# A macaron block on one core: wide products whose result nothing reads, x loaded twice, the last numerators without DRAM

## The chip, the core and the metric

The kernel is one program on one NeuronCore of a Trainium2 chip. The metric is the device time of one execution, in microseconds (us). A profile of one execution gives the start and length of each instruction; times inside it are counted from the start of the span.

## The reference

x is (4, 1024, 128) in float32, so there are 4096 tokens of 128 numbers. Three layers add to x in turn:

```python
x = x + 0.5 * ffn(layernorm(x))
x = x + attn(layernorm(x))
x = x + 0.5 * ffn(layernorm(x))

def ffn(x):                       # 8 experts, each token goes to one
    top1 = argmax(softmax(x @ router_w + router_b))
    for i in range(8):
        a, g = split(x @ w1[i] + b1[i])          # 128 -> 2 x 512
        y = (a * sigmoid(g)) @ w2[i] + b2[i]     # 512 -> 128
        out += where(top1 == i, y, 0)
    return out

def attn(x):                      # 16 heads of 8, scores plus phi_bias
    p = softmax(q @ k.T * 8**-0.5 + log(exp(-|pos_i - pos_j|) + 1e-8))
    return (p @ v) @ w_proj + b_proj
```

## The kernel before

The work is in five parts, one after another on the core: the first routing (`phase_first`), the first experts, the preparation of attention (`phase_attend`), attention (`phase_attention_last`, 64 heads; its end holds the second routing), and the second experts. Both experts parts are `phase_experts`. Each engine has a program of its own, and semaphores order them.

**Routing.** The 4096 tokens are 32 tiles of 128, taken as 8 groups of 4 tiles (512 tokens) and 4 chunks of 2 groups. For a group, VectorE takes mean and variance, ScalarE (for some groups VectorE) writes the normalised tokens into `xn`, TensorE turns four tiles (`turn`), ScalarE copies them to `xT`, and TensorE multiplies them with the router's weights, which are only 8 columns wide (`use`, L275). For a chunk, VectorE picks each token's expert in a row of small dependent steps with drains between them; TensorE counts the tokens above each token (`rank_chunk`, L285 and L287); VectorE writes two arrays of marks (L242 and L251), and TensorE sums them in eight products into a table of which token stands in which place (`enter_chunk`, L305). The last chunk's steps are `Router.place_last`, which gives its marks in two halves. `count_tokens` (L293) gives the tokens of each expert; `plan_tiles` turns these into the 39 tiles of the experts part: starts of experts, `slot`, `eid`, and, when ScalarE has copied the table (`copy_table`, L314) and TensorE has picked from it (`pick_tokens`, L323), the token numbers `idx`. The gathers of the experts part wait for `idx` and for all stores of `stored` (`load_first_rows`). ScalarE's queue holds `halve_bias` (L373) in front of `copy_table`; it waits until all expert weights and `b2` have landed. `run_up` (L380) is RUNUP products of 128x256 float32 that nothing reads, after the pick. A product in float32 shows as two instructions in the trace.

**Rows and DMA.** `g.rows` keeps 256 numbers per token: the normalised token, and behind it x (`g.xt`). A store to DRAM takes both together (`store_rows`, L98). In `phase_first`, x is loaded straight into `g.xt`, that is in pieces of 512 bytes: groups 0, 1, 2 and 3, 6 and 7 by SyncE's queue, 4 and 5 by ScalarE's. Then SyncE issues the marks, and group by group the weights `w1` and `w2` of an expert and the store of the group's rows, each store after the group is normalised, and last `b2`. The second routing has the same loop, without the loads of x.

**The end of attention.** Two heads at a time end in `osum` in SBUF (32-row blocks: 8 rows of numerators and one denominator for each quarter of the tokens; two heads side by side). SyncE writes them to `weighted_sums` in DRAM and later reads numerators (`load_num`) and denominators (`load_den`) of a batch back in the layout that the projection needs. For the last two heads the denominators already go from `osum` to `den` directly (`load_last_den`, L1055). Their numerators go to DRAM (L1232), SyncE waits for that, and reads them back (L1061). VectorE multiplies numerators and reciprocals (`divide_last`, L1503) for groups 6 and 7, TensorE projects (`project`, L1375), VectorE adds to x (`new_x`, L1508), and the routing steps of groups 6 and 7 follow. The chunks 1, 2 and 3 of the second routing lie behind that in VectorE's program.

## Time and profile before

| what | value |
|---|---|
| time, median of 3 runs | 1059.32 us (1057.64 to 1061.11) |
| the profiled execution's own time | 1058.07 us |
| its span, first to last instruction | 1056.2 us |
| TensorE busy | 977.1 us, 93% |
| VectorE busy | 899.5 us, 85% |
| ScalarE busy | 734.5 us, 70% |
| GpSimd busy | 357.5 us, 34% |
| DMA | 102.40 MB, mean 97 GB/s |

The first routing runs from the start of the span to about 52 us, the second from about 892 us to about 937 us. Busy shares are means over the whole span; the routing stages are read by themselves from the timeline.

### The profile page before, as it was taken

The numbers are of one execution on the slowest core, as the hardware profiler recorded it, in microseconds if no ns is written. First come the engines' busy times: TensorE is split into PE (matmuls) and PEld (weight loads), VectorE is DVE, ScalarE is ACT, GpSimd is POOL, SyncE is SP. The second block draws the span as 40 slices with busy tenths as digits, with TensorE's granted clock in tenths as the row PEclk, the third lists the DMA queues.
The fourth block names the chain that finished last, engine by engine and source line by source line (L and its number), as shares of the span: only waits on it lengthen the run. The fifth ranks groups of instructions, "written<-read, shape, count | busy, mean of one in ns | idle before, by whom it ended". The sixth has DMA issues, their size and how long they took to land. (4 is left out here: it accounts for less than half of the span.)

```text
span 1056.2 us, 34555 instructions
## 1 busy us (share of the span) xinstructions
PE 977.1 (93%) x11722; PEld 544.9 (52%) x11722; DVE 899.5 (85%) x1638; ACT 734.5 (70%) x1587; POOL 357.5 (34%) x495
## 2 busy tenths in 40 slices
PE   5899995969999999999999999999999989679997
PEld 4799993513333333333333333333333335569997
DVE  6778874779999999999999999999999988667886
ACT  4244442848888888888888888888888875234443
POOL 0067772202222222223222232222222242027775
PEclk9999996969999999999999999999999999679999
DMA  9532224752222222222222222222222343922221
GB/s 323 206 96 70 70 70 112 241 192 65 70 76 63 70 72 60 73 71 64 72 69 69 63 73 74 59 73 72 58 74 71 100 121 98 336 81 70 70 71 41
DMA packets 77898, 102.40 MB, mean 97 GB/s; under 512 B 15473, under 2 KB 55031, under 8 KB 77798
## 3 DMA queue, kind: packets, MB, share of 16 engines
q1 hardware_dynamic: 67830, 84.21, 26.6%
q0 software_dynamic: 6240, 14.44, 4.6%
q10 hardware_dynamic: 3760, 2.89, 0.9%
q8 instruction: 37, 0.61, 0.2%
q14 instruction: 31, 0.25, 0.1%
HBM read 70.61 MB, written 31.78 MB: 97 GB/s over the span
## 5 line engine op out<-in xcount | busy, mean ns | idle before, releaser
L1490 DVE TENSOR_REDUCE nmax<-psS 128x1 f32<-128x1024 f32 x507 | 595.7, 1218 | 36.7 <-PE psS L1326 29.3
L1672 ACT ACTIVATE big<-psE 128x512 f32<-128x512 f32 x1024 | 553.4, 598 | 95.6 <-PE psE L1311 93.1
L1311 PE MATMUL psE<-qop,kop 122*32 122x512 bf16 x4096 | 318.0, 384 | 5.0 <-ACT big L1672 3.6
L1761 POOL TENSOR_TENSOR big<-big,const 128x512 f32<-128x512 f32 x128 | 139.8, 1092 | 464.7 <-ACT big L1672 464.7
L1346 PE MATMUL psV<-big,vst 128*9 128x256 f32 x4096 | 265.6, 379 | 1.3
L1326 PE MATMUL psS<-maxop 32*128 32x512 bf16 x1014 | 174.6, 391 | 20.6 <-DVE nmax L1490 12.1
L1346 PEld LDWEIGHTS psV<-big,vst 128*9 128x9 f32 x4096 | 101.8, 90 | 116.3 <-issue 12.6
L1311 PEld LDWEIGHTS psE<-qop,kop 122*32 122x32 bf16 x4096 | 90.2, 95 | 130.7 <-ACT big L1672 59.5
L1326 PEld LDWEIGHTS psS<-maxop 32*128 32x128 bf16 x1014 | 47.7, 91 | 179.3 <-issue 109.1
L1028 ACT ACTIVATE sigb<-psGb,big 128x128 f32<-128x128 f32 x156 | 44.6, 368 | 59.2 <-PE psGb L953 59.2
L1028 ACT ACTIVATE siga<-psGa,w1sa 128x128 f32<-128x128 f32 x156 | 44.6, 369 | 58.4 <-PE psGa L953 58.4
L119 POOL DMA_INDIRECT xs<-stored_a,idx x39 | 38.1, 977 | 60.8 <-ACTq L386 49.2
L119 POOL DMA_INDIRECT xs<-stored_b,idx x39 | 38.0, 974 | 57.8 <-DVE idx L357 46.3
L930 POOL DMA_INDIRECT out_x<-yb,idx x39 | 44.3, 1136 | 25.7 <-issue 13.0
L930 POOL DMA_INDIRECT results<-ya,idx x39 | 44.9, 1151 | 23.7 <-issue 11.4
L1011 DVE SCALAR_TENSOR_TENSOR hidb<-psAb,big,sigb 128x128 f32<-128x128 f32 x156 | 43.6, 342 | 2.2 <-PE psAb L953 2.0
L1011 DVE SCALAR_TENSOR_TENSOR hida<-psAa,w1sa,siga 128x128 f32<-128x128 f32 x156 | 43.7, 342 | 1.0 <-ACT siga L1028 0.8
L969 PE MATMUL psYa<-w2a,hida 128*128 x312 | 41.5, 276 | 1.7 <-DVE hida L1011 1.6
L969 PE MATMUL psYb<-big,hidb 128*128 x312 | 41.6, 276 | 1.6 <-DVE hidb L1011 1.6
L953 PE MATMUL psGb<-xsTb,big 128*128 128x128 f32 x312 | 42.3, 280 | 0.7 <-ACT xsTb L1036 0.7
L953 PE MATMUL psGa<-xsTa,w1sa 128*128 128x128 f32 x312 | 41.5, 276 | 0.7 <-ACT xsTa L1036 0.7
L953 PE MATMUL psAb<-xsTb,big 128*128 128x128 f32 x312 | 42.0, 279 | 0.0
(213 smaller groups left out, 940.0 us busy)
## 6 DMA issues: line engine op xcount, KB each, us to landing
maxop<-qk_parts SPq DMA_DIRECT2D x256, 64.0 KB, 1.9
qop<-qk_parts SPq DMA_DIRECT2D x64, 144.0 KB
kop<-qk_parts SPq DMA_DIRECT2D x64, 144.0 KB
weighted_sums<-osum SPq DMA_DIRECT2D x64, 128.0 KB
qk_parts<-big SPq DMA_DIRECT2D x12, 384.0 KB, 3.4
w1a<-in_w SPq DMA_DIRECT2D x8, 516.0 KB, 7.6
big<-in_w SPq DMA_DIRECT2D x8, 516.0 KB, 6.9
stored_a<-rows SPq DMA_DIRECT2D x8, 512.0 KB, 7.7
```

Source lines behind the costliest of these rows:

```text
L119: pool.indirect_dma_start(out=g.xs[:, i % XBUF, :], out_offset=None, in_=d.stored[g.turn], in_offset=bass.IndirectOffsetOnAxis(ap=g.idx[:, ...
L930: pool.indirect_dma_start(out=to, in_=y[:, s, :], in_offset=None, bounds_check=NTOK - 1, oob_is_err=False, out_offset=bass.IndirectOffsetO ...
L953: last = nc.tensor.matmul(ps[:, c * P:(c + 1) * P], w1s[:, s, lo:lo + P], xsT[:, s, :], start=True, stop=True)
L969: last = nc.tensor.matmul(psY[1 - s][:, 0:D], hid[:, 1 - s, c * P:(c + 1) * P], g.w2[:, bass.ds(e * HID + c * P, P)], start=(c == 0), stop ...
L1011: last = nc.vector.scalar_tensor_tensor(out=hid[:, s, c * P:(c + 1) * P], in0=psA[s][:, c * P:(c + 1) * P], scalar=w1s[:, s, 2 * HID + c:2 ...
L1028: last = nc.scalar.activation(sig[:, s, c * P:(c + 1) * P], psG[s][:, c * P:(c + 1) * P], ACT.Sigmoid, bias=w1s[:, s, b:b + 1])
L1311: last = nc.tensor.matmul(psE[BANK[turn]][32 * c:32 * c + 32, :], kop[b][0:TROWS, lo:lo + 32], qop[b][0:TROWS, half * HALF:(half + 1) * HALF],
L1326: last = nc.tensor.matmul(psS[n % 2][:, half, :], maxop[b][lo:lo + SROWS, 0, qt % 4 * P:(qt % 4 + 1) * P], maxop[b][lo:lo + SROWS, 1, :], ...
L1346: last = nc.tensor.matmul(psV[32 * c:32 * c + VW, side:side + QUART], vst[(r + 1) % 2][:, k, :], prob[(r + 1) % 2][:, at_c:at_c + QUART], ...
L1490: nc.vector.tensor_reduce(nmax[r % 2][:, qt:qt + 1], psS[n % 2][:], AX.XY, ALU.max, negate=True).then_inc(s_max, 1)
L1672: nc.scalar.activation(prob[r % 2][:, lo:lo + HALF], psE[BANK[16 * (r % NBUF) + n]][:], ACT.Exp).then_inc(s_exp, 1)
L1761: nc.gpsimd.tensor_tensor(dst, dst, diag[:, 4 * h:4 * h + 4, :], ALU.mult).then_inc(s_diag, 1)
```

## The change

Five things change.

- **Unread products.** TensorE gets more products of 128x256 float32 whose result nothing reads. In the first routing: 7 at the start (on an array `fill` of zeros that GpSimd writes), one after each of 8 turns, one after each of 7 uses, then 2, 1, 4 and 1 around the last counts and table entries: 30. In the second: 13, on constants. RUNUP goes from 5 to 7.
- **Early x.** Groups 0 to 3 are loaded into an array `xq` of their own, in pieces of 2 KB or more, and are read from there. All loads of x are in SyncE's queue, the constants in one load behind groups 0 and 1. Behind the marks, the x of groups 0 to 3 is loaded again into `g.xt` (1 MB), and the store of group 0 waits for that.
- **Last numerators.** `load_last_num` moves the last two heads' numerators from `osum` to `num`, four DMAs by SyncE and four by GpSimd; `divide_last(7)` waits for GpSimd's. The last write to `weighted_sums`, the wait for it and the read back are gone.
- **Counting inside place_last.** Six small steps of `plan_tiles` (up to `at`) stand between the steps of `place_last`, which now holds `rank`, `near` and `split` too, and a wait for the counts.
- Waits of TensorE for constants are one, behind the first 7 products.

```diff
@@ -50,7 +50,8 @@
...
 LEAD = 2
-RUNUP = 5
+RUNUP = 7
+EARLY = 4
@@ -252,17 +253,30 @@
...
-    def place_last(self, dve, c):
+    def place_last(self, dve, c, p):
...
         h = CT // 2
+        self.rank(c)
+        dve.drain()
+        dve.wait_ge(p.s_cnt, 1)
+        self.near(c)
+        self.v.tensor_scalar(p.near[:, 0:E], p.counts[:, 0:E], float(P - 1) / 2, MAGIC, ALU.add, ALU.add)
+        self.v.memset(p.pad[:, 0:1], 0.0)
+        dve.drain()
+        self.split(c)
+        self.v.tensor_scalar(p.pad[:, 1:E + 1], p.near[:, 0:E], -MAGIC, None, ALU.add)
+        dve.drain()
...
         self.one_column(c)
+        self.v.tensor_tensor_scan(p.start[:], self.g.const[:, C_ONE:C_ONE + E + 1], p.pad[:], 0.0, ALU.mult, ALU.add)
...
         self.name(c)
+        self.v.tensor_tensor(p.mine[:, 0:E], p.start[:, 0:E], self.g.const[:, C_MASK:C_MASK + E], ALU.mult)
...
         dve.drain()
+        self.v.tensor_reduce(p.at[:], p.mine[:, 0:E], AX.X, ALU.add)
@@ -327,18 +341,6 @@
...
-    dve.wait_ge(p.s_cnt, 1)
-    nc.vector.tensor_scalar(p.near[:, 0:E], p.counts[:, 0:E], float(P - 1) / 2, MAGIC, ALU.add, ALU.add)
-    nc.vector.memset(p.pad[:, 0:1], 0.0)
-    dve.drain()
-    nc.vector.tensor_scalar(p.pad[:, 1:E + 1], p.near[:, 0:E], -MAGIC, None, ALU.add)
-    dve.drain()
-    nc.vector.tensor_tensor_scan(p.start[:], g.const[:, C_ONE:C_ONE + E + 1], p.pad[:], 0.0, ALU.mult, ALU.add)
-    dve.drain()
-    nc.vector.tensor_tensor(p.mine[:, 0:E], p.start[:, 0:E], g.const[:, C_MASK:C_MASK + E], ALU.mult)
-    dve.drain()
-    nc.vector.tensor_reduce(p.at[:], p.mine[:, 0:E], AX.X, ALU.add)
-    dve.drain()
@@ -402,7 +404,9 @@
...
             sem(n) for n in ("var", "std", "rs", "xn", "xa", "tp", "xT", "used"))
-        s_upto, s_rank, s_small, s_marks, s_ident = (sem(n) for n in ("upto", "rank", "small", "marks", "ident"))
+        s_upto, s_rank, s_small, s_marks, s_again, s_fill = (
+            sem(n) for n in ("upto", "rank", "small", "marks", "again", "fill"))
+        xq, fill = sb("xq", [P, 4 * EARLY, D]), sb("fill", [P, OFFS])
@@ -419,20 +423,30 @@
...
+        def load_early(eng, n, count):
+            eng.dma_start(xq[:, 4 * n:4 * (n + count), :].rearrange("p j d -> p (j d)"),
+                          d.x[:, n * HALF:(n + count) * HALF]).then_inc(s_src[n], 16)
+        def x_of(t):
+            return xq[:, t, :] if t < 4 * EARLY else xt[:, t, :]
...
         def _(sp):
-            load_x(sp, 0, 1)
-            sp.dma_start(g.const[:, 0:C_TRI], d.const[:, 0:C_TRI]).then_inc(s_ident, 16)
-            load_x(sp, 1, 1)
-            sp.dma_start(g.const[:, C_TRI:C_DIAG], d.const[:, C_TRI:C_DIAG]).then_inc(s_small, 16)
-            load_x(sp, 2, 2)
+            load_early(sp, 0, 1)
+            load_early(sp, 1, 1)
+            sp.dma_start(g.const[:, 0:C_DIAG], d.const[:, 0:C_DIAG]).then_inc(s_small, 16)
+            load_early(sp, 2, 2)
+            load_x(sp, 4, 2)
...
             sp.dma_start(g.marks[:], d.marks).then_inc(s_marks, 16)
+            sp.dma_start(xt[:, 0:EARLY * 4, :], d.x[:, 0:EARLY * HALF].rearrange("p (j d) -> p j d", d=D))\
+                .then_inc(s_again, 16)
...
                 if n == 0:
+                    sp.wait_ge(s_again, 16)
@@ -441,13 +455,14 @@
...
         def _(pool):
+            nc.gpsimd.memset(fill[:], 0.0).then_inc(s_fill, 1)
...
                 for j in range(lo, hi):
-                    nc.vector.bn_stats(stats[:, c, j, :], xt[:, CT * c + j, :])
+                    nc.vector.bn_stats(stats[:, c, j, :], x_of(CT * c + j))
@@ -466,7 +481,7 @@
...
                 for j in range(4):
-                    last = nc.vector.tensor_scalar(xn[:, j, 0:D], xt[:, j, :], mv[:, 0, j, 0:1], rstd[:, 0, j:j + 1],
+                    last = nc.vector.tensor_scalar(xn[:, j, 0:D], x_of(j), mv[:, 0, j, 0:1], rstd[:, 0, j:j + 1],
@@ -503,6 +518,9 @@
...
                 dve.drain()
+                if t == CHUNKS:
+                    router.place_last(dve, t - 1, plan)
+                    break
@@ -527,9 +545,6 @@
...
                     router.pick(t)
-                if t == CHUNKS:
-                    router.place_last(dve, t - 1)
-                    break
@@ -559,9 +574,16 @@
...
         def _(pe):
+            def unread(count, bank):
+                for _ in range(count):
+                    nc.tensor.matmul(bank[:, 0:OFFS], fill[:, 0:P], fill[:], start=True, stop=True)
+            pe.wait_ge(s_fill, 1)
+            unread(7, plan.counts)
+            pe.wait_ge(s_small, 3 * 16)
...
                 if n == 0:
-                    pe.wait_ge(s_ident, 16)
@@ -570,12 +592,13 @@
...
                 last.then_inc(s_tp, 1)
+                unread(1, plan.counts)
...
             def use(n):
-                if n == 0:
-                    pe.wait_ge(s_small, 3 * 16)
...
                 use_group(nc, pe, router, xT, n).then_inc(s_used, 1)
+                if n < groups - 1:
+                    unread(1, plan.counts)
@@ -596,10 +619,14 @@
...
             enter_chunk(nc, pe, router, 1)
+            unread(2, psT[1])
...
             count_tokens(nc, pe, router, plan)
+            unread(1, psT[1])
             enter_chunk(nc, pe, router, 2)
+            unread(4, psT[1])
             enter_chunk(nc, pe, router, 3)
+            unread(1, psT[1])
@@ -607,13 +634,12 @@
...
             act.dma_start(g.br[:], d.router_b.partition_broadcast(P)).then_inc(s_small, 16)
-            load_x(act, 4, 2)
...
                     k = n % 2 * 4 + j
-                    last = nc.scalar.activation(xn[:, 4 * n + j, 0:D], xt[:, 4 * n + j, :], ACT.Identity,
+                    last = nc.scalar.activation(xn[:, 4 * n + j, 0:D], x_of(4 * n + j), ACT.Identity,
@@ -1055,6 +1081,16 @@
...
+def load_last_num(eng, g, osum, quarters, landed):
+    for c in quarters:
+        for side in range(2):
+            lo = (HEADS - 2 + side) * DH
+            eng.dma_start(g.num[lo:lo + DH, (B - 1) % 2, c * QUART:(c + 1) * QUART],
+                          osum[32 * c:32 * c + DH, side * QUART:(side + 1) * QUART]).then_inc(landed, 16)
@@ -1148,7 +1184,7 @@
...
         s_aT_last = m.sem("s_aT_late")
-        s_pick, s_spread = m.sem("s_pick"), m.sem("s_spread")
+        s_pick, s_spread, s_num_late = m.sem("s_pick"), m.sem("s_spread"), m.sem("s_num_late")
@@ -1226,7 +1262,8 @@
...
                             load_last_den(sp, g, osum[s], side)
-                    for side in range(2):
+                        load_last_num(sp, g, osum[s], (0, 1), g.s_num_in[B - 1])
+                    for side in range(2 if at != N + 1 else 0):
@@ -1277,8 +1314,6 @@
...
             steps(sp, step, -3, N + 2)
-            sp.wait_ge(s_os[1], 16 * (N // 2))
-            load_num(sp, d, g, B - 1, HEADS - 2, HEADS)
@@ -1429,6 +1464,11 @@
...
             steps(pe, step, -2, N + 1)
+            def unread(count):
+                for _ in range(count):
+                    nc.tensor.matmul(psD[0][:, 0:OFFS], g.const[:, C_ONE:C_ONE + P], g.const[:, 0:OFFS],
+                                     start=True, stop=True)
@@ -1441,22 +1481,31 @@
...
             turn(4)
+            unread(1)
...
             use(4)
+            unread(1)
             use(5)
+            unread(2)
...
             pe.wait_ge(s_ev, N // 2)
+            unread(1)
...
             turn(6)
+            unread(1)
...
             use(6)
+            unread(1)
...
             enter_chunk(nc, pe, router, 1)
+            unread(2)
...
             enter_chunk(nc, pe, router, 2)
+            unread(3)
             enter_chunk(nc, pe, router, 3)
+            unread(1)
@@ -1497,7 +1546,9 @@
...
                 if n % 2 == 0:
-                    dve.wait_ge(g.s_num_in[B - 1], 2 * 16)
+                    dve.wait_ge(g.s_num_in[B - 1], 5 * 16)
+                else:
+                    dve.wait_ge(s_num_late, 4 * 16)
@@ -1580,6 +1631,9 @@
...
                 dve.drain()
+                if place == CHUNKS - 1:
+                    router.place_last(dve, place, plan)
+                    return
@@ -1601,9 +1655,6 @@
...
                 dve.drain()
-                if place == CHUNKS - 1:
-                    router.place_last(dve, place)
-                    return
@@ -1794,6 +1845,8 @@
...
             steps(pool, step, -1, 64)
+            pool.wait_ge(s_ev, N // 2)
+            load_last_num(pool, g, osum[(N // 2 - 1) % 2], (2, 3), s_num_late)
...

```

## Rows read from the trace of the kernel before

**Rows 1.** The page's slices of the span (40 of 26.4 us): TensorE's granted clock in tenths.

```profile
PEclk9999996969999999999999999999999999679999
```

**Rows 2.** Busy time by stretch, first routing: us, PE, PEld, DVE, ACT, POOL, PEclk, DMA share, GB/s.

```profile
4.00:10.00 6.00, 0.00 (x0) 0.00 (x0) 3.57 (x23) 0.41 (x2) 0.00 (x0) 1.00 1.06 302
10.00:39.00 29.00, 26.86 (x123) 24.69 (x124) 22.47 (x122) 15.87 (x39) 0.00 (x0) 1.00 1.03 398
```

**Rows 3.** Timeline, first routing, VectorE: start us, us, what [idle before, releaser].

```profile
7.70 0.88 DVE L450 BATCH_NORM_STATS2 stats_first<-rows 128x6 f32<-128x128 f32 x4 [2.10 <-DMA rows<-in_x]
```

**Rows 4.** Waits of VectorE in the first 52 us: total, times, longest.

```profile
DVE row_first L211 <- PE psL_first L287: 2.2, 3, 0.9
```

**Rows 5.** Timeline, end of the first routing and first experts tile.

```profile
40.63 1.06 ACT L373 ACTIVATE b2a<-b2a 128x1024 f32<-128x1024 f32 x1 [8.19 <-DMA b2a<-in_b]
...
44.91 1.93 PE L305 MATMUL psI_first<-hot_off_first,hot_col_first 128*128 128x256 f16 x8 [1.98 <-DVE hot_col_first L251]
...
45.28 0.17 DVE L331 TENSOR_SCALAR near_first<-psC_first 128x8 f32<-128x8 f32 x1
45.40 0.06 DVE L332 MEMSET pad_first<- 128x1 f32 x1
...
46.87 0.37 ACT L314 CAST table_first<-psI_first 128x256 f16<-128x256 f32 x1 [5.18 <-PE psI_first L305]
...
52.75 0.30 PE L961 MATMUL psXa<-const,xs 128*128 128x128 f32 x1 [1.06 <-DMA xs<-stored_a,idx]
...
55.86 1.13 DVE L1011 SCALAR_TENSOR_TENSOR hida<-psAa,w1sa,siga 128x128 f32<-128x128 f32 x4 [0.82 <-ACT siga L1028]
```

**Rows 6.** Groups by form, first 52 us, then 919 to 921 us: busy us, mean ns.

```profile
L275 PEld LDWEIGHTS psL_first<-wr,xT_first 128*128 128x128 f32 x64 | 14.1, 332 | 0.3 <-ACT xT_first L624 0.2
...
L380 PE MATMUL psI_first<-const 128*128 128x256 f32 x10 | 4.3, 613 | 0.0
...
L275 PEld LDWEIGHTS psE<-wr,xT_last 128*128 128x128 f32 x16 | 1.9, 191 | 0.0
```

**Rows 7.** Timeline, end of attention and start of the second routing.

```profile
892.23 2.05 PE L1375 MATMUL psS<-wproj,aT 128*128 128x128 f32 x16
...
892.98 1.33 SPq L1055 DMA_DIRECT2D den<-osum  x2
...
895.90 0.95 DVE L1496 RECIPROCAL rec<-den 128x128 f32<-128x128 f32 x1 [0.23 <-DMA den<-osum]
...
899.22 0.69 SPq L1061 DMA_DIRECT2D num<-weighted_sums  x1
...
904.18 1.28 DVE L1503 TENSOR_TENSOR aT<-num,psE 128x512 f32<-128x512 f32 x2 [5.40 <-DMA num<-weighted_sums]
...
904.92 3.50 PE L1375 MATMUL psS<-wproj,aT 128*128 128x128 f32 x16 [5.17 <-DVE aT L1503]
...
907.03 0.69 DVE L1508 TENSOR_TENSOR rows<-psS,rows 128x512 f32<-128x512 f32 x1 [0.91 <-PE psS L1375]
```

**Rows 8.** The page's groups: gathers issued by GpSimd, busy us, mean ns of one.

```profile
L119 POOL DMA_INDIRECT xs<-stored_a,idx x39 | 38.1, 977 | 60.8 <-ACTq L386 49.2
```

**Rows 9.** Busy time by stretch, second routing and start of the experts (columns as in rows 2).

```profile
904.00:927.00 23.00, 17.01 (x95) 14.90 (x96) 19.97 (x84) 7.27 (x17) 0.00 (x0) 0.65 1.02 396
...
935.30:938.70 3.40, 1.52 (x8) 0.88 (x6) 0.76 (x2) 0.27 (x1) 2.67 (x3) 1.00 0.26 77
938.70:942.10 3.40, 3.40 (x16) 3.40 (x17) 1.04 (x2) 1.14 (x4) 1.97 (x2) 0.50 0.37 96
```

**Rows 10.** Timeline, end of the second routing and first tile of the second experts.

```profile
929.23 1.06 ACT L373 ACTIVATE big<-big 128x1024 f32<-128x1024 f32 x1 [9.07 <-DMA big<-in_b]
...
932.31 0.37 ACT L314 CAST table_last<-psV 128x256 f16<-128x256 f32 x1 [2.02 <-PE psV L305]
...
937.97 0.30 PE L961 MATMUL psXb<-const,xs 128*128 128x128 f32 x1 [1.52 <-DMA xs<-stored_b,idx]
...
942.34 1.12 DVE L1011 SCALAR_TENSOR_TENSOR hidb<-psAb,big,sigb 128x128 f32<-128x128 f32 x4 [1.99 <-PE psAb L953]
```


## The prediction

> **What bounds the kernel now.** I read the page's slices first, then the two routing stretches by themselves, since the change touches only those. Between them TensorE is granted its full clock nearly everywhere [rows 1] and nothing is edited there. In the page's slices both routings look like a mix; the timeline shows one chain in each.
>
> First routing. Three things run side by side. The DMA engines are full from 4 to 39 us, at 302 GB/s up to 10 us, where x arrives in 512-byte pieces, and at 398 GB/s after it [rows 2]. VectorE is busy 22.47 of the 29 us from 10 to 39 and most of the rest is drains between short dependent steps; the waits that the profile names are 2.1 us for the second piece of x [rows 3] and 2.2 us for TensorE's ranks [rows 4]. TensorE is busy 26.86 of those 29 us [rows 2]. The granted clock says 1.00 there, but nothing had been recorded yet: a weight load of L275 takes 332 ns, and 191 ns in the second routing at a time when the clock was granted in full [rows 6]. So I read the whole first routing as run at 1.2 GHz.
>
> The stretch ends at ScalarE's copy of the table, at 46.87, and from there to the first turn of the experts, at 52.75, is a fixed tail of 5.9 us [rows 5]. What came last was the table (1.93 us of eight products from 44.91). But ScalarE's queue has a second gate: the halved bias waits for `b2`, the last weight to land, until 40.63 and takes 1.06 us. So the DMA side ends at 41.7, which leaves 5.2 us of slack [rows 5]. This is the number to watch.
>
> Second routing. VectorE stops for 5.40 us (898.8 to 904.18) for the last heads' numerators, which SyncE could ask for only at 899.22; TensorE stops with it for 5.17 us and then projects at 1.2 GHz, 3.50 us instead of the 2.05 us of the same sixteen instructions at 892.23 [rows 7]. After that VectorE is busy 19.97 of 23 us [rows 9], so it sets the pace up to the last marks. DMA is again full, 396 GB/s from 904 to 927 [rows 9], the bias is released at 929.23 and done at 930.3, and the copy follows at 932.31: only 2.0 us of slack [rows 10].
>
> **The last numerators.** Before, the denominators took 1.33 us for two issues from 892.98, and the reciprocal ran at 895.90, 1.6 us after the second issue ended [rows 7]. Four more issues by SyncE at 0.67 us each end at 897.0 and land at 898.6 by the same 1.6 us. GpSimd's four have no row of their kind; the nearest is its gathers, 977 ns each [rows 8]: 892.98 + 3.9 = 896.9, landed 898.5 by the same 1.6 us, or 900.5 if each took half as long again. VectorE is free at 898.8 and TensorE at 899.75 (904.92 less its wait of 5.17) [rows 7]. So the projection starts at 899.8 instead of 904.92, 5.1 us sooner, and at the higher clock the first half is done 0.7 us sooner still (half of 3.50 less 2.05). `new_x(6)` moves from 907.03 to 901.2, 5.8 us sooner. GpSimd has nothing else to do there; were its landing at 900.5, only group 7 would be late, by some 1 us, and VectorE with it.
>
> The DMA side moves less. SyncE's first weights come behind its last `num` issue: 897.0 instead of 899.9 (899.22 + 0.69) [rows 7], 2.9 us sooner, with the same bytes behind them. `b2` then releases ScalarE at 926.3 and the bias is done at 927.3 [rows 10]. The compute chain would ask for the copy at 932.31 - 5.8, plus the counting steps and less a faster table (both below, +0.7 and -0.5), about 926.7. So DMA comes last, by 0.6 us, and the second routing gains 932.31 - 927.3 = **5.0 us**. Bounds: 3 us (GpSimd late, TensorE at 1.2 GHz) and 6.3 us (no DMA limit).
>
> **Early x.** x of groups 0 and 1 no longer shares the queues with ScalarE's 512 KB, so most of the 2.1 us wait [rows 3] goes. Its first 1 MB in long pieces I take at 398 instead of 302 GB/s: 0.9 us saved (2.6 for 3.5). The second load of that 1 MB is in 512-byte pieces: 3.5 us at 302 GB/s, 2.6 at 398. And SyncE now holds the store of group 0 and all that follows until it has landed; what is queued meanwhile is one expert's weights (772 KB) and the padding, some 2.3 us of work, against an estimated 3 us for a landing to be seen and a new issue to reach the engines (twice the 1.6 us above): a hole of 0 to 1 us, 0.5 taken. Together the DMA side of the first routing gets 3.1 us later: bias released at 43.7, done at 44.8. The compute side gains up to 2.1 + 2.2 us, so it would ask for the copy at 46.87 - 4.3 + 0.2 = 42.8. DMA comes last again, now by 2.0 us: the first routing gains 46.87 - 44.8 = **2.1 us**. Bounds: 0.5 us (hole of 1 us, TensorE slower) and 4.1 us (DMA not in the way).
>
> By the fit in the Trainium skill, DMA: Bandwidth & Descriptors, Anatomy of one DMA, 1.05 MB costs 2.4 us beyond the fixed part; with that the gain here would be 1.1 us larger. The rows at 302 GB/s speak for the dearer price.
>
> **The unread products.** One is two instructions, and ten took 4.3 us at the lower clock [rows 6], 0.86 each, 0.43 to 0.5 at the higher one (by the ratio of 332 to 191 and by half). The first seven run before any data is there, 6 us at most, and TensorE did nothing before 10 us [rows 2]. The next fifteen, in turns and uses, cost 6.5 to 7.5 us at 2.4 GHz, while L275's loads alone fall from 14.1 to 8.1 us [rows 6]; the other products, nearly half of the busy time, save an estimated 3. So at the high clock TensorE has slightly less to do than before, and its short answers to VectorE (ranks) come sooner: the 2.2 us of rows 4, if not all. The four before the last marks fill a wait of 1.98 us [rows 5] with 1.7 to 2.0 us at the high clock; the one behind the last table entries lies beside ScalarE's copy and the DMA wait: nothing. The second routing's thirteen cost 5.6 to 6.5 us, in 6.0 us of idle time [rows 9], beside work that gets faster than its mean clock of 0.65. Eight table products at the high clock I take as 1.0 of 1.93 us, 0.5 on the path because the second half waits for its marks.
>
> **The counting.** Six small steps stand in `place_last` instead of behind it. One more step costs 0.12 us (45.28 to 45.40) [rows 5]: +0.7 us before the last marks; the drains they stood between are there already. Behind the marks 1.2 us go, but those lay beside the 1.93 us of table products. So +0.7 and nothing back, unless TensorE is fast: then `slot` would have been the next thing late. With DMA last in both routings, neither shows.
>
> **The run-up.** Seven products take 3 us at the high clock instead of 4.3 for five. They end at about 48 in the first routing, 2.3 us before the first gather (52.75 - 2.1 = 50.6). In the second routing of before, a run-up that had reached the high clock ended at 936.45, 1.52 us before the first turn (937.97), and the clock fell at 938.7 for 3.4 us [rows 9, 10]. The first tile then took 942.34 - 937.97 = 4.4 us up to VectorE's product; in the first experts, at the high clock, 55.86 - 52.75 = 3.1 us [rows 5]. I expect the fall in both now: **+1.3 us** for the first experts, 0 for the second, which had it.
>
> **Sum.** -5.0 - 2.1 + 1.3 = -5.8 us. Against the profiled execution's own 1058.07: 1052.3. The median of the runs shown lies 1.25 us above that execution and the runs spread over 3.5 us; I put the after median at 1052.5.
>
> **Rivals.**
> A. DMA is not what comes last (the early pieces save more, the hole does not appear). Compute sets both ends: 4.1 and 5.6, with or without the 1.3: 1048.4 or 1049.7. For: the bias starts 1.6 us after DMA is full for the last time (39 us [rows 2]), so landing times as well as bytes decide. Against: bytes only grow. 0.17.
> B. The first routing gives nothing: the 1 MB read again and SyncE's wait take all 5.2 us of slack. -5.0 + 1.3: 1054.4; with a late GpSimd too (gain 3), 1056.4. 0.2 for the two.
> C. Slower: the clock stays at 1.2 GHz in spite of the products. The first routing has fifteen at 0.86 = 12.9 us in a TensorE that had 2.1 us idle [rows 2]; less 2.1 for x and the 4 us of slack that the forecast leaves between it and VectorE's chain of before, some +7. The second has 11.2 us for 6.0 idle, +5, and gives back its 5.0. About 1065; in between, it decides from the point where half the turns and uses run low. For: in the second routing a mean of 0.65 [rows 9] is what today's mix gets, and the products of `fill` are zeros, of which no row exists. Against: after the ten instructions of the old run-up [rows 6] the first experts already went at the high clock (their first tile above), and fifteen products spread out keep TensorE as long as all of L275. 0.07.
> The Trainium skill, TensorE: Matmul & The Clock Gate, PE-mode transpose, says that transposes do not count as activity for the clock. That would leave the turns to the new products alone and speaks for C; the fall at 938.7 behind a single turn fits it but does not show it.
> D. The edits hide where other work covers them: within 0.3% of before. 0.06.
>
> **Chances and range.** My forecast 0.5 (its own range 1050 to 1055), A 0.17, B 0.2, C 0.07, D 0.06. The range 1047.5 to 1056.5 holds all but C, D and the end of B. 0.3% is 3.2 us, about what a measurement of this kernel can tell from none. Faster than 1056.1: forecast, A, most of B, 0.83; within 0.3%: D and the end of B, 0.1; slower: 0.07.
>
> **What would show it.** In the profile after: no wait of VectorE for DMA before `divide_last`; projection at about 899.8 less the first routing's gain; L275's loads near 191 ns in the first routing; the bias (L373) ending just before the table's copy in both routings; the second piece of x not waited for; a clock of 0.5 for 3.4 us after both run-ups. Wrong: L275 still at 332 ns (C), the copy well behind the bias (compute last), GpSimd's landing after 900, or the bias of the first routing released before 42 or after 46.

## The result, and the profile after

The changed kernel takes 1050.13 us in the median of 4 runs (1048.93 to 1050.75), before 1058.48 us in the same measurement (4 runs). The ratio is 0.9921, with a 95% interval of 0.9903 to 0.9939. The forecast was 1052.5, with a range of 1047.5 to 1056.5. The profiled execution took 1050.04 us, its span is 1048.2 us, 8.0 us shorter than before.

The page's slices mix too much to show either routing, so the reading is again by stretch. Timeline, first routing, the lines that answer to [rows 3] and [rows 5]:

```profile
5.92 0.87 DVE L465 BATCH_NORM_STATS2 stats_first<-xq_first 128x6 f32<-128x128 f32 x4 [0.50 <-DMA xq_first<-in_x]
...
8.99 3.14 SPq L114 DMA_DIRECT2D stored_a<-in_padding  x1
...
15.85 0.33 SPq L99 DMA_DIRECT2D stored_a<-rows  x1
...
16.88 0.23 DVE L170 TENSOR_TENSOR logit_first<-psL_first,br 128x64 f32<-128x64 f32 x1 [1.30 <-PE psL_first L289]
...
43.39 1.16 PE L319 MATMUL psI_first<-hot_off_first,hot_col_first 128*128 128x256 f16 x8 [1.39 <-DVE hot_col_first L252]
...
45.24 1.06 ACT L375 ACTIVATE b2a<-b2a 128x1024 f32<-128x1024 f32 x1 [13.52 <-DMA b2a<-in_b]
46.20 0.35 ACT L328 CAST table_first<-psI_first 128x256 f16<-128x256 f32 x1
...
51.74 0.30 PE L987 MATMUL psXa<-const,xs 128*128 128x128 f32 x1 [1.79 <-DMA xs<-stored_a,idx]
```

The second piece of x is waited for 0.50 us instead of 2.10. The table's eight products end at 44.55, but the copy stands at 46.20, right behind the bias, which the last weight releases only at 45.24 instead of 40.63. SyncE shows a part of where the time went: its padding store takes 3.14 us to issue behind the second load's many pieces, and the first store of rows goes out at 15.85, where before it went at 10.48. So the first routing won 1.0 us, not more.

Busy time by stretch (us, PE, PEld, DVE, ACT, POOL, PEclk, DMA share, GB/s), to set beside [rows 2]:

```profile
6.00:9.50 3.50, 1.51 (x9) 1.09 (x8) 3.27 (x20) 0.67 (x3) 0.00 (x0) 1.00 1.07 340
9.50:19.70 10.20, 9.62 (x36) 8.04 (x35) 7.11 (x48) 6.21 (x17) 0.00 (x0) 0.50 1.05 329
19.70:46.00 26.30, 22.27 (x154) 19.35 (x152) 20.95 (x92) 9.95 (x23) 0.00 (x0) 1.00 0.92 361
```

Here the clock is on record from 9.5 us. The seven products at the start had raised it to 2.4 GHz: the four turns at 8.82 take 0.63 us, while the first four take 1.09 us in a kernel without the products (no_unread below). It was lost again within 3.5 us in which TensorE was busy 1.51, and the routing went on at 1.2 GHz up to 19.7, with the products in the turns and uses and at their dear price. After that it held. The form of L275's line (now L289) in two of these stretches, 10 to 20 us and 20 to 35 us (busy us, mean ns), confirms how [rows 6] were read:

```profile
L289 PEld LDWEIGHTS psL_first<-wr,xT_first 128*128 128x128 f32 x16 | 3.9, 334 | 0.4
...
L289 PEld LDWEIGHTS psL_first<-wr,xT_first 128*128 128x128 f32 x48 | 6.3, 192 | 0.3
```

The second routing, timeline, answering to [rows 7] and [rows 10]:

```profile
890.10 0.59 ACT L1731 COPY osum<-psV 128x512 f32<-128x512 f32 x1 [2.85 <-PE psV L1381]
890.71 1.26 SPq L1081 DMA_DIRECT2D den<-osum  x2
890.98 2.16 POOL L1090 DMA_DIRECT2D num<-osum  x4 [4.48 <-ACT osum L1731]
...
892.01 2.72 SPq L1090 DMA_DIRECT2D num<-osum  x4
...
894.77 0.92 SPq L104 DMA_DIRECT2D big<-in_w  x2
...
896.14 1.29 DVE L1554 TENSOR_TENSOR aT<-num,psE 128x512 f32<-128x512 f32 x2
...
898.35 0.69 DVE L1559 TENSOR_TENSOR rows<-psS,rows 128x512 f32<-128x512 f32 x1 [0.26 <-PE psS L1410]
...
914.40 0.23 DVE L170 TENSOR_TENSOR logit_last<-psE,br 128x64 f32<-128x64 f32 x1 [1.24 <-PE psE L289]
...
923.73 1.07 ACT L375 ACTIVATE big<-big 128x1024 f32<-128x1024 f32 x1 [10.86 <-DMA big<-in_b]
...
925.13 0.37 ACT L328 CAST table_last<-psV 128x256 f16<-128x256 f32 x1 [0.34 <-PE psV L319]
...
930.57 0.30 PE L987 MATMUL psXb<-const,xs 128*128 128x128 f32 x1 [1.68 <-DMA xs<-stored_b,idx]
```

`divide_last` waits for no DMA any more. Behind it VectorE waits for the logits from TensorE (1.24 us), and the bias is done (924.80) just before the table. The granted clock of this routing is 0.50 from about 903.8 to 910.6 and from 920.8 to 924.2, and 1.00 otherwise.

From such lines of the timeline comes one table of all kernels. The first two columns are times; "middle" is from psXa to the copy of osum (which no edit touches); the next columns count from that copy; "rest" is from psXb to the end of the span.

| kernel | copy 1 | psXa | middle | aT | new_x(6) | bias | copy 2 | psXb | rest |
|---|---|---|---|---|---|---|---|---|---|
| before | 46.87 | 52.75 | 839.61 | 11.82 | 14.67 | 36.87 | 39.95 | 45.61 | 118.23 |
| after | 46.20 | 51.74 | 838.36 | 6.04 | 8.25 | 33.63 | 35.03 | 40.47 | 117.63 |
| num_alone | 47.63 | 53.47 | 839.31 | 6.10 | 8.25 | 34.16 | 35.81 | 41.50 | 116.92 |
| num_by_dram | 46.33 | 51.85 | 839.04 | 11.31 | 14.16 | 36.39 | 39.29 | 44.67 | 117.64 |
| no_unread | 46.36 | 51.87 | 839.20 | 6.05 | 8.25 | 33.09 | 34.08 | 39.56 | 116.17 |
| x_direct | 44.68 | 50.20 | 839.33 | 6.05 | 8.25 | 34.03 | 34.99 | 40.38 | 117.49 |
| count_behind | 46.83 | 52.50 | 839.52 | 6.06 | 8.25 | 34.16 | 35.12 | 40.49 | 117.89 |
| bias_last | 44.87 | 50.35 | 839.62 | 6.21 | 8.25 | - | 34.87 | 40.26 | 117.47 |
| bias_last_no_unread | 45.03 | 50.54 | 839.37 | 6.05 | 8.25 | - | 36.20 | 41.63 | 116.16 |
| pool_copy_bias_last | 45.90 | 51.45 | 839.64 | 6.04 | 8.25 | - | 33.30 | 38.71 | 116.10 |
| pool_copy_bias_last_again | 45.08 | 50.59 | 839.73 | 6.10 | 8.25 | - | 33.32 | 38.74 | 116.64 |
| pool_copy_bias_last_no_unread | 45.23 | 50.85 | 838.22 | 6.27 | 8.31 | - | 36.25 | 41.71 | 116.12 |
| x_direct_no_unread_bias_last | 45.25 | 50.79 | 838.76 | 6.05 | 8.25 | - | 36.18 | 41.68 | 116.17 |
| pool_copy_bias_last_count_behind | 44.45 | 50.99 | 841.59 | 6.05 | 8.25 | - | 33.10 | 39.32 | 116.70 |

One of the six executions of x_direct took 1762.22 us, the other five 1049.26 to 1051.01, and its ratio is without that one.

Before to after: first routing -1.01, middle -1.25, second routing -5.14, rest -0.60, together -8.0 us. The middle and the rest are not edited, only the run-ups ahead of them. They spread over 3.4 us (838.22 to 841.59) and 2.1 us (116.10 to 118.23) between kernels whose code there is the same, so 1.85 of the 8.0 us are not claimed for the change.

### The profile page after: what moved, and what is told of

The parts are those of the page before. It is cut to its first block and busy times, and to the rows that moved or that the text cites. A ratio compares the mean times of both kernels' runs of the same rounds, so it can differ in the third digit from the quotient of the medians.

```text
span 1048.2 us, 34735 instructions
## 1 busy us (share of the span) xinstructions
PE 979.2 (93%) x11813; PEld 551.0 (53%) x11816; DVE 897.2 (86%) x1638; ACT 732.7 (70%) x1587; POOL 360.7 (34%) x500
## 5 line engine op out<-in xcount | busy, mean ns | idle before, releaser
L1361 PE MATMUL psS<-maxop 32*128 32x512 bf16 x1014 | 171.8, 390 | 23.1 <-DVE nmax L1539 13.7
L956 POOL DMA_INDIRECT out_x<-yb,idx x39 | 44.7, 1147 | 25.0 <-issue 11.6
```

What stands on the lines that cost most here:

```text
L956: pool.indirect_dma_start(out=to, in_=y[:, s, :], in_offset=None, bounds_check=NTOK - 1, oob_is_err=False, out_offset=bass.IndirectOffsetO ...
L1361: last = nc.tensor.matmul(psS[n % 2][:, half, :], maxop[b][lo:lo + SROWS, 0, qt % 4 * P:(qt % 4 + 1) * P], maxop[b][lo:lo + SROWS, 1, :], ...
```

## The experiments

Two questions are asked: which edit carries the gain, and what stands last at the end of each routing, the table's products or the bias ahead of its copy in ScalarE's queue. All are timed against the kernel before in the same measurement. Unless said otherwise, "the full change" is the kernel after.

**num_alone.** The kernel before, with `load_last_num` and nothing else:

```diff
+                        load_last_num(sp, g, osum[s], (0, 1), g.s_num_in[B - 1])
...
+            load_last_num(pool, g, osum[(N // 2 - 1) % 2], (2, 3), s_num_late)
...
-            load_num(sp, d, g, B - 1, HEADS - 2, HEADS)
```

> The kernel before with the direct numerators alone. Theory N (the gain is the removed wait for the numerators, about 5.1 us in the second routing, whatever the other edits do): 4.5 to 5.5 us below before, some 3 us above the full change. With the clock of before TensorE projects at the high clock, since it no longer stops, so new_x(6) should come near 6 us sooner and the bias (L373), released about 3 us sooner, should be what the table's copy waits for. Rival W (the unread products carry the gain by keeping the clock up): at most 2 us below before.

Measured 1052.86 us, ratio 0.9941 (0.9922 to 0.9961), so 6.3 us of 1059.54, more than the 4.5 to 5.5 of theory N; rival W, at most 2, falls. One of five edits gives the greater part of the gain. aT comes at 6.10 us as in the full change, and the second routing is 4.1 us shorter; part of the rest of the 6.3 is the rest of the kernel, where its second experts are 1.3 us shorter. One expected sign did not come: the bias is released 2.7 us sooner behind osum, but the second copy waits 0.59 us for the table, not for the bias. The interval overlaps that of the full change, so this run by itself does not show that the other edits add anything.

**num_by_dram.** The full change with that one edit undone.

```diff
-                        load_last_num(sp, g, osum[s], (0, 1), g.s_num_in[B - 1])
...
+            load_num(sp, d, g, B - 1, HEADS - 2, HEADS)
```

> The full change with the last numerators through DRAM again; all else of the change is kept. Theory N: VectorE stops again for the read back, aT 11.8 us behind the copy of osum instead of 6.0, the bias 3 us later, so 4.5 to 6 us above the full change, 3 to 4 us below before. Rival W (the products keep the clock up through the stop and win back the slower projection and more): at most 3.5 us above the full change.

Measured 1055.7 us, ratio 0.9963 (0.9949 to 0.9976): 3.9 us below before, 4.5 us above the full change by the two ratios, (0.9963 - 0.9921) x 1060. VectorE's timeline:

```profile
902.20 1.28 DVE L1553 TENSOR_TENSOR aT<-num,psE 128x512 f32<-128x512 f32 x2 [5.21 <-DMA num<-weighted_sums]
```

The stop is back with 5.21 us. Theory N holds from both sides. The interval ends below 1, so the other edits together do give something without this one.

**no_unread.** `range(count)` in both `unread` helpers becomes `range(0)`, and RUNUP 5.

> The full change without any of its 43 unread products, and RUNUP back at 5. Theory G (in both routings the bias, that is the last weights' landing, or VectorE's own chain sets the end; in the second routing of the full change VectorE even waits 1.24 us for TensorE behind a product): within 1 us of the full change, so 7.5 to 9 us below before. In the first routing the copy would stand right behind the bias again. Rival W (the products are worth what the clock is worth): 3 to 4 us above the full change. A fallen clock at the start of either experts part would cost 1.3 us and is counted apart.

Measured 1049.53 us, ratio 0.9910 (0.9893 to 0.9927): the same as the full change. All 43 products and the two of each run-up can go without a loss that shows in the total. Timeline of ScalarE in both routings:

```profile
45.40 1.06 ACT L375 ACTIVATE b2a<-b2a 128x1024 f32<-128x1024 f32 x1 [14.48 <-DMA b2a<-in_b]
46.36 0.35 ACT L328 CAST table_first<-psI_first 128x256 f16<-128x256 f32 x1
...
924.16 1.06 ACT L375 ACTIVATE big<-big 128x1024 f32<-128x1024 f32 x1 [11.89 <-DMA big<-in_b]
925.15 0.37 ACT L328 CAST table_last<-psV 128x256 f16<-128x256 f32 x1
```

In both, the copy follows the bias without a gap and waits for no product: the gate decides. A point that matters further down: in the second routing the last eight table products start 32.11 us behind osum here (923.18), and 33.67 in the full change (923.77), so VectorE's chain is no later without the products.

```profile
923.18 1.93 PE L319 MATMUL psV<-hot_off_last,hot_col_last 128*128 128x256 f16 x8 [2.00 <-DVE hot_col_last L252]
```

**x_direct.** x is loaded once, in 512-byte pieces, in the new order, all by SyncE; no second load.

```diff
-EARLY = 4
+EARLY = 0
...
-            load_early(sp, 0, 1)
+            load_x(sp, 0, 1)
...
-            sp.dma_start(xt[:, 0:EARLY * 4, :], d.x[:, 0:EARLY * HALF].rearrange("p (j d) -> p j d", d=D))\
-                .then_inc(s_again, 16)
...
-                    sp.wait_ge(s_again, 16)
```

> The full change with x loaded once, straight into the rows in 512-byte pieces, all in SyncE's queue, in the new order, and no second load. Theory G: 1 MB less ahead of the weights, so the bias is released near 41.5 instead of 45.24; the second piece of x comes up to 2 us later, so the table is complete near 45 to 46.5. The two nearly cancel: within 0.7 us of the full change. Rival X (early pieces are worth their 2 us): 1.5 to 2 us slower than the full change.

Measured 1049.88 us, ratio 0.9914 (0.9894 to 0.9933): the same. ScalarE's timeline:

```profile
40.65 1.06 ACT L375 ACTIVATE b2a<-b2a 128x1024 f32<-128x1024 f32 x1 [8.85 <-DMA b2a<-in_b]
...
44.68 0.37 ACT L328 CAST table_first<-psI_first 128x256 f16<-128x256 f32 x1 [2.97 <-PE psI_first L319]
```

The bias is released at 40.65, as before the change, and the copy waits for the table. So the second load and SyncE's wait for it cost the DMA side 4.6 us, and the end of the routing 1.5 (psXa at 50.20 instead of 51.74). The total does not show these 1.5 us beyond its interval. Theory G (within 0.7 us) holds and rival X falls. The stretch from 18 to 22 us shows a part of the 4.6, first in the full change, then here:

```profile
18.00:22.00 4.00, 4.00 (x26) 3.61 (x24) 3.59 (x24) 2.43 (x6) 0.00 (x0) 0.79 0.89 256
```

```profile
18.00:22.00 4.00, 4.00 (x25) 3.61 (x23) 3.68 (x24) 2.32 (x6) 0.00 (x0) 0.78 1.03 416
```

The DMA engines move 256 GB/s behind SyncE's wait and 416 without it, which is 0.64 MB or 1.5 us less. The second load's 1.05 MB at 416 GB/s is another 2.5 us.

**count_behind.** The counting steps go back behind the last marks.

> The full change with the counting steps back behind the last marks, as before. Theory P (each small step ahead of the last marks costs 0.12 us and the steps behind them lie beside the table): the last marks come 0.6 to 0.7 us sooner, the slots 0.6 us later than the copy; in the first routing the bias at 45.24 hides both, in the second the slots come last: within 0.5 us of the full change. Rival Q (the move shortens the tail by its 1.2 us): 1 to 2 us above the full change, with the slots (L344 of the full change) behind the table's copy in both routings.

Measured 1051.69 us, ratio 0.9926 (0.991 to 0.9942), against 0.9921: the same, and rival Q (1 to 2 us above) is not shown. Both copies stand behind the bias again. Theory P gave 0.6 to 0.7 us for the last marks of the second routing, but their products start 31.95 us behind osum for 33.67; the granted clock differs too (1.00 nearly throughout here), so this pair does not price the steps.

**bias_last.** Two lines change places, in both routings.

```diff
+            copy_table(nc, act, router)
             halve_bias(nc, act, g)
-            copy_table(nc, act, router)
```

> The full change with the bias halved behind the table's copy instead of ahead of it, in both routings. Theory G: in the first routing the table is complete at 44.55 and the copy stood at 46.20, so the copy comes 1.6 us sooner; in the second it waited 0.34 us for the table, nothing to win: 1.3 to 1.9 us below the full change. Rival S (the gathers wait for the stores anyway, which land with the weights): same as the full change, with GpSimd's first gather waiting for the stores instead of idx.

Measured 1049.19 us (1045.27 to 1051.12), ratio 0.9895 (0.9871 to 0.9919). Timeline:

```profile
44.87 0.37 ACT L328 CAST table_first<-psI_first 128x256 f16<-128x256 f32 x1 [12.87 <-PE psI_first L319]
45.35 1.06 ACT L375 ACTIVATE b2a<-b2a 128x1024 f32<-128x1024 f32 x1
```

The first copy comes 1.3 us sooner and psXa 1.4 us, near theory G, and the gathers follow, which rival S denied. But the intervals of the two ratios overlap, and its executions fall near 1045.3 twice and between 1048.8 and 1051.1 four times.

**bias_last_no_unread.** As the last, without the products.

> The full change without its 43 unread products, RUNUP 5, and with the bias behind the copy, so that nothing but the table, the slots and VectorE set the end. This asks whether the products were worth nothing only because the bias hid them. Theory G2 (what the higher clock saves TensorE, the products spend again): same as the kernel with the bias last alone, within 1 us, that is 1048 to 1050, 9 to 11 us below before. Rival W2 (the products do shorten the chain once it decides): 1.5 to 3 us above the kernel with the bias last alone.

Measured 1048.96 us, ratio 0.9902 (0.9883 to 0.9922): no difference that can be told from bias_last in the total, so here theory G2 holds and rival W2 does not, although the bias stands in nobody's way. In the stages there are two that cancel: the second copy at 36.20 us behind osum instead of 34.87, and a shorter rest, 116.16 for 117.47. With the products the granted clock falls to 0.50 in the first tile of the second experts, without them it stays at 1.00.

**x_direct_no_unread_bias_last.** Only the direct numerators and the counting inside `place_last` are left of the change, and the bias is last.

> A simpler kernel: the direct numerators and the counting inside place_last are kept; x is loaded once in 512-byte pieces, there are no unread products, RUNUP is 5, and the bias stands behind the copy. Theory G2: 1048 to 1050.5, as fast as the full change or up to 2 us faster. Rival W2 or X (products and early pieces are each worth 1 to 2 us): 1052 or more.

Measured 1049.35 us (1049.25 to 1049.67), ratio 0.9906 (0.9888 to 0.9925). A kernel without products, `xq` and the second load is as fast as the full change, as G2 has it (1048 to 1050.5).

**pool_copy_bias_last.** The bias last; x of groups 0 to 3 goes from `xq` to the rows by GpSimd instead of a second load.

```diff
-            sp.dma_start(xt[:, 0:EARLY * 4, :], d.x[:, 0:EARLY * HALF].rearrange("p (j d) -> p j d", d=D))\
-                .then_inc(s_again, 16)
...
+                if n < EARLY:
+                    sp.wait_ge(s_again, n + 1)
...
-                    sp.wait_ge(s_again, 16)
...
+            for n in range(EARLY):
+                if n in s_src:
+                    pool.wait_ge(s_src[n], 16)
+                nc.gpsimd.tensor_copy(xt[:, 4 * n:4 * n + 4, :], xq[:, 4 * n:4 * n + 4, :]).then_inc(s_again, 1)
```

> The full change with the bias last, and with GpSimd copying x of groups 0 to 3 from xq into the rows in SBUF instead of the second load from DRAM. DMA then ends near 40 instead of 43 us, but the table sets the end already, at 44.9. Theory C (compute chain decides): same as with the bias last alone, within 0.5 us. Rival D (the gathers or the tokens' stores are late by DMA): 1 us or more below it.

Measured 1045.55 us (4 runs), ratio 0.9868 (0.9849 to 0.9886), the fastest median. Theory C (within 0.5 us of bias_last) misses by the medians, 3.6 us, but the intervals of the two overlap, and no wait for DMA that rival D could rest on is shown. Its four executions are few, so a second measurement follows.

**pool_copy_bias_last_again.**

> The fastest kernel so far once more, since its four executions (1045.1 to 1047.8) were few and the one with the bias last alone spread from 1045.3 to 1051.1: 1045 to 1049 if the gain over the full change holds, 1049 or more if it was the luck of the clock.

Measured 1047.46 us (1046.97 to 1048.98), ratio 0.9885 (0.9869 to 0.9901). It is faster than the full change: both intervals, 0.9849 to 0.9886 and 0.9869 to 0.9901, end below the 0.9903 at which that of the full change begins, the second only just. By the ratios the gain over the full change is (0.9921 - 0.9885) x 1060 = 3.8 us or (0.9921 - 0.9868) x 1060 = 5.6 us. Its place is only partly shown: the first copy comes 0.3 to 1.1 us sooner, the second 1.7, at 33.3 us behind osum. In the full change the first stood behind the bias, the second behind the table by 0.34 us. That GpSimd's copy gives anything is not shown: against bias_last the first copy is no sooner (45.90 and 45.08, there 44.87), and in the second routing, where the copy comes 1.6 us sooner than in bias_last, GpSimd's move of x has no part. Those 1.6 us are VectorE's: in bias_last it waits 1.22 us for TensorE's logits, behind a granted clock of 0.50, and here it does not. Nor does it in x_direct, whose last table products start 32.15 us behind osum, for 32.11 and 32.13 here and 33.67 in bias_last. So the edit is not needed for it.

**pool_copy_bias_last_no_unread.**

> GpSimd's copy of early x, the bias last, no unread products, RUNUP 5. In the kernels so far the table's copy of the first routing came at 44.7 to 45.3 us with and without the products. Theory G2: within 1.5 us of the same kernel with the products (1045.6), and the copy of the first routing at 44.5 to 45.5. Rival W2: 2 us or more above it, 1047.6 or later, for the second routing, where the last marks came 31.6 to 33.2 us behind osum with the products and 31.6 to 33.8 without.

Measured 1049.67 us, ratio 0.9905 (0.989 to 0.992): 2.1 us (by the second measurement of the kernel with products) to 3.9 us (by the first) above it. Rival W2 holds here and theory G2 falls, though the interval is clear only of the first measurement's (0.9886), not of the second's (0.9901). Busy time by stretch of the second routing, first the kernel with the products (again), then this one:

```profile
907.00:920.00 13.00, 10.43 (x69) 8.82 (x69) 11.27 (x50) 2.82 (x6) 0.00 (x0) 0.89 1.03 414
```

```profile
907.00:920.00 13.00, 10.46 (x48) 8.77 (x46) 9.77 (x40) 2.15 (x5) 0.00 (x0) 0.50 1.03 416
```

TensorE is busy equally long, but with 69 instructions at a granted 0.89 in one and 48 at 0.50 in the other, and VectorE, which has the same program, gets through 50 of its instructions instead of 40. But a low clock alone does not do that. The same stretch of no_unread, which has no products either:

```profile
907.77:920.77 13.00, 10.55 (x57) 8.38 (x56) 11.28 (x50) 2.82 (x6) 0.00 (x0) 0.63 1.03 415
```

VectorE gets through 50 there too, at a granted 0.63, and does not wait for the logits. The last eight table products show the price of the clock (timeline, same order):

```profile
922.45 1.15 PE L319 MATMUL psV<-hot_off_last,hot_col_last 128*128 128x256 f16 x8
```

```profile
923.35 1.93 PE L319 MATMUL psV<-hot_off_last,hot_col_last 128*128 128x256 f16 x8 [1.99 <-DVE hot_col_last L252]
```

The second copy comes at 33.32 with the products and at 36.25 without. That is 2.9 us: 0.8 are the table products themselves (1.93 for 1.15), 2.15 their later start (34.28 behind osum for 32.13). The first part follows the clock. The second is not safely the products': they start at 32.11 in no_unread, without products, and at 33.67 in bias_last, with them. In the first routing the products show nothing: the copy comes at 45.23 without them, 45.08 and 45.90 with them. With the bias ahead of it the copy could not have come before the bias was done, at 34.1 to 35.2 (the table's column plus 1.0), so most of the 2.9 us would not have shown there. That the products were worth nothing in the full change because another gate decided fits this pair of kernels; bias_last and bias_last_no_unread, where that gate is gone as well, do not bear it out in the total.

**pool_copy_bias_last_count_behind.** The same kernel with the counting behind the last marks.

> GpSimd's copy of early x, the bias last, and the counting steps back behind the last marks, so that no gate hides them. Theory P: the last marks 0.7 us sooner, but the slots (and with them the pick, idx and the gathers) some 1.5 us behind the last marks instead of 0.1: 0 to 0.7 us above the kernel with the counting moved. Rival Q: 1.2 us or more above it.

Measured 1050.18 us (1045.74 to 1051.16), ratio 0.99 (0.9883 to 0.9917). Timeline:

```profile
44.45 0.37 ACT L315 CAST table_first<-psI_first 128x256 f16<-128x256 f32 x1 [12.50 <-PE psI_first L306]
...
44.85 0.26 DVE L343 TENSOR_SCALAR slot_first<-const,at_first 128x78 f16<-128x78 f32 x1
...
45.26 0.21 PE L324 MATMUL psT_first<-slot_first,table_first 128*128 128x39 f16 x2 [0.42 <-DVE slot_first L343]
...
46.92 0.20 DVE L358 TENSOR_TENSOR idx<-above_first,none_first 128x39 int32<-128x39 f32 x1
```

Now the pick waits for the slots, and idx comes 2.47 us behind the copy, where the kernel with the counting moved needs 1.39 (46.47 - 45.08). The copy itself is 0.6 us sooner in the first routing and 0.2 in the second (33.10). Net 0.6 us in psXb (39.32 against 38.74) and 0.4 in psXa (50.99 against 50.59), about 1 us. The medians lie 2.7 us apart, the ratios 1.6 us, and the intervals overlap. Of the profiled executions' difference 1.9 us is in the middle (841.59 for 839.73). Its code is the same, but it is not clear of the edit: the run-up ends 2.41 us before the first turn instead of 1.75, and the granted clock is then 0.50 from about 50.7 to 57.5 us, where the other kernel has it from 51.3 to 54.7. Theory P (0 to 0.7 us) and rival Q (1.2 or more) both had the sign; the stages' 1 us lies between them, and the totals nearer to Q. Neither is decided.

## Why the prediction was right, step by step

- **The last numerators: right, nearly to the tenth.** In time from osum, the forecast had the first weights of SyncE at 897.0 - 892.36 = 4.6 us (measured 4.67), the projection at 7.4 (7.07), new_x(6) at 8.8 (8.25), the bias released at 33.9 (33.63) and the copy at 34.9 (35.03). The gain of the second routing was 5.0 in the forecast and 5.14 in the profile. GpSimd's four issues took 2.16 us together, not 3.9: the gathers were the wrong neighbour, but its share was hidden.
- **Two gates at once in the second routing: right in the sum, for a mixed reason.** I had DMA last by 0.6 us. The table came last, by 0.34, because VectorE's chain lost 1.24 us to TensorE (the wait at 914.40, behind turns, uses and products partly at 1.2 GHz); I had counted the products into idle time. Whether the products are to blame is not shown: x_direct has them and no such wait, num_alone has none of them and waits 1.55 us. This forecast error was nearly hidden by the bias in the same place.
- **Early x: right about what decides, mis-sized.** The bias gates the copy, as forecast. But it was released at 45.24, not 43.7: second load and wait cost 4.6 us instead of 3.1. The hole behind SyncE's wait is the part that was too small, 0.5 us in the forecast and 1.5 by the stretch from 18 to 22 us (256 GB/s for 416): the first store went out 5.4 us later than before, and one issue of SyncE stood for 3.14 us. The 0.9 us counted for the long pieces cannot be seen either: from 2 to 18 us the engines moved 302 GB/s, before 313. The routing gained 1.0 us instead of 2.1. The fit in the Trainium skill, DMA: Bandwidth & Descriptors, Anatomy of one DMA, is one of transfers that GpSimd issues; by it the bytes alone, 1.05 MB, are an estimated 2.4 us. That agrees with 2.5 us at the 416 GB/s of this trace, and the measured 4.6 us hold the hole as well. The compute side asked for the copy at 44.7 to 44.9 (x_direct, bias_last) and not at 42.8. The clock of 1.2 GHz from 9.5 to 19.7 is the likely reason, but no run varies it alone.
- **The unread products: worth nothing in the change as it stands, as forecast** (no_unread). With the bias out of the way one pair of kernels shows 2.1 to 3.9 us for them and another none, so what they are worth by themselves stays open. And the clock was not simply high: it was lost for 10 us in the first routing and for 6.8 and 3.4 us in the second.
- **The counting: right that it would not show** (count_behind). Where nothing hides it, it seems to give about 1 us in the stages, which is within the noise of the total.
- **The fall of the clock before the first experts: did not come** in the profiled execution; the term of +1.3 us was the wrong one. The granted clock stayed 1.00 up to 159 us, though the first tile took 3.99 us for 3.1 because VectorE waited for the next tile's gather. In other kernels it did fall there (bias_last, num_alone and all with GpSimd's copy and the products, for example). In the second experts it fell from 931.1 to 934.5, as forecast. In the eight profiles where it stayed up there the rest is 116.1 to 116.9 us, in those where it fell 117.5 to 118.2, which fits the 1.3 us priced from [rows 9, 10]. It fell in five of the eight profiles with the products and in none of the five edited kernels without them (in the kernel before it did), so a part of what the products give may be lost again here. With one profile of each kernel it cannot be told whether this goes by kernel or by execution.
- **Rival C's price was mis-added.** 12.9 - 2.1 of idle time - 2.1 for x - 4 of slack is 4.7 us, not 7, so C stood at about 1063, not 1065. Its premise came true for ten of the first routing's microseconds; its time did not.
- **Sum.** -5.0 became -5.14, -2.1 became -1.0, +1.3 became 0, and -1.85 came from stretches that no edit touches: -8.0 instead of -5.8. Against the profiled execution the forecast was 2.2 us too high (1052.3 for 1050.04), and by terms: second routing -0.1, first routing +1.1, the fall of the clock -1.3, stretches with the same code -1.9. The two edited routings were forecast 0.9 us too good together, and what made up for it more than fully is outside them. That part of the nearness is luck.
- **Open.** What the unread products are worth by themselves, what makes the fastest kernel the fastest (GpSimd's copy is not shown to), and how much of the differences below 2 us between kernels is the clock's chance.

## What to carry to other kernels

When a stage ends where two chains meet, here a table and the landing of the last weight, write down when each is ready before pricing an edit: most of these edits worked on the chain that was about to come second. In the first routing they brought the first turn of the experts 1.0 us forward, and moving one line in ScalarE's queue another 1.4. A load that has to be read back from DRAM only because of its layout is the better target: one wait of 5.4 us gave the greater part of the gain (4.5 to 6.3 us of 8.3). Work that only keeps the clock up should be tried again each time a gate goes, and by more than one pair of kernels: the same 43 products gave nothing in two pairs (no_unread, bias_last_no_unread) and 2 to 4 us in a third.

## What was not expected of the hardware

GpSimd issues a plain move of 8 KB between places in SBUF in 0.54 us (four in 2.16), about half of one of its gathers (977 ns, [rows 8]). The clock raised by the products at the start was lost again in 3.5 us in which TensorE was busy 1.51, and did not come back for 10.2 us although TensorE was then busy 9.62 of them.
